# A one-core transformer layer with a mixture of experts: every token through every expert, or sorted rows through 72 expert tiles

## The reference

```python
scores = sigmoid(xf @ gate_w.T)                       # 8 experts
topk_w, topk_idx = top_k(scores, 2)
topk_w = topk_w / (topk_w.sum(-1) + 1e-20) * 2.5
shared_out = silu(xf @ shared_wg.T) * (xf @ shared_wu.T) @ shared_wd.T       # hidden width 352
h = silu(einsum('td,efd->etf', xf, exp_wg)) * einsum('td,efd->etf', xf, exp_wu)
all_out = einsum('etf,edf->etd', h, exp_wd)           # hidden width 176 per expert, all 8 experts
routed_out = (topk_w[..., None] * picked).sum(1)      # the two chosen of all_out
x = x + shared_out + routed_out
```

## Time and profile before

| | us |
|---|---|
| three runs, median (lowest to highest) | 6289.63 (6270.85 to 6297.65) |
| profiled execution, span from the first to the last instruction | 6271.0 |
| expert stage in it, 5590 to the end | 681 |
| of this: normalise, transpose, route | 5590 to 5630 |
| shared blocks | 5630 to 5766 |
| routed blocks | 5766 to 6271 |

### The profile page before, as it was taken

The page is one execution under the profiler, slowest core; times in us unless marked ns, Lnnn a source line. Parts: engine busy times, 40 slices in busy tenths (PEclk is TensorE's granted clock), DMA queues, the critical chain, the costliest instruction groups (busy, mean ns, idle before and its releaser), DMA issues. The chain is left out here.

```text
span 6271.0 us, 142359 instructions
## 1 busy us (share of the span) xinstructions
PE 4569.4 (73%) x49630; PEld 2127.3 (34%) x49630; DVE 5470.7 (87%) x7473; ACT 4790.6 (76%) x6674; POOL 4595.8 (73%) x3263
## 2 busy tenths in 40 slices
PE   7656666766667666666666667676666666899999
PEld 3422222222222222222222222222222224565555
DVE  8889999999999999999999999999999995543222
ACT  5469899998998898989998899898998993541010
POOL 4568888888888888888888888888888883530000
PEclk9889999999999999999999999999999998989999
DMA  4267777777777777777777777777777771010000
GB/s 126 66 125 144 137 142 144 140 143 138 146 143 139 140 146 140 142 146 140 142 142 157 140 143 140 141 142 138 143 144 143 140 145 45 0 36 0 9 8 10
DMA packets 2231975, 735.90 MB, mean 117 GB/s; under 512 B 2175765, under 2 KB 2209400, under 8 KB 2225561
## 3 DMA queue, kind: packets, MB, share of 16 engines
q1 hardware_dynamic: 2196249, 576.08, 45.2%
q0 software_dynamic: 35456, 157.33, 14.1%
HBM read 168.97 MB, written 27.26 MB: 31 GB/s over the span
## 5 line engine op out<-in xcount | busy, mean ns | idle before, releaser
L911 DVE TENSOR_SCALAR_CACHE_REDUCE scores<-ring,step 128x2048 f32<-128x2048 f32 (+2 forms) x2560 | 4780.0, 1919 | 51.5 <-PE ring L838 39.2
L970 ACT ACTIVATE n_op<-scores,bias 128x2048 uint8<-128x2048 f32 x2048 | 4075.9, 1997 | 279.0 <-DVE m_rest L918 278.8
L786 POOL CAST nT<-pairs 128x2048 f16<-128x2048 uint8 x2048 | 3790.9, 1890 | 515.9 <-DMA pairs<-n_op 504.8
L838 PE MATMUL ring<-x_all,q_op 128*128 128x512 bf16 x8192 | 2226.2, 385 | 652.9 <-DVE scores L911 589.1
L838 PEld LDWEIGHTS ring<-x_all,q_op 128*128 128x128 bf16 x8192 | 682.6, 98 | 1857.8 <-DVE scores L911 1186.2
L835 PE MATMUL ring<-x_all,q_op 128*128 128x512 bf16 x2048 | 628.8, 389 | 723.1 <-DVE scores L911 707.0
L850 PE MATMUL pO<-nT,v_op 128*32 128x128 f16 x32768 | 656.1, 223 | 148.4 <-ACT att_g L988 109.1
L850 PEld LDWEIGHTS pO<-nT,v_op 128*32 128x32 f16 x32768 | 479.4, 97 | 596.1 <-issue 513.4
L1760 ACT ACTIVATE h_gate<-pGt 128x512 f32<-128x512 f32 (+1 forms) x112 | 66.9, 597 | 528.3 <-PE pWt L1701 433.6
L835 PEld LDWEIGHTS ring<-x_all,q_op 128*128 128x128 bf16 x2048 | 116.6, 97 | 994.9 <-DVE scores L911 977.7
L970 ACT ACTIVATION_READ_ACCUMULATOR n_op<-scores,bias 128x1 f32 x2048 | 395.7, 193 | 0.0
(11 more groups left out here) (201 smaller groups left out, 3366.1 us busy)
## 6 DMA issues: line engine op xcount, KB each, us to landing
x_all<-keys_transposed POOLq DMA_DIRECT2D x128, 768.0 KB, 8.5
v_st<-value_integers POOLq DMA_DIRECT2D x128, 256.0 KB, 3.5
pairs<-n_op SPq DMA_TRANSPOSE x2048, 2.7
keys_transposed<-kT_s POOLq DMA_DIRECT2D x32, 384.0 KB, 3.3
cT<-in_ctx_T SPq DMA_DIRECT2D x32, 256.0 KB, 2.7
q_op<-queries_transposed POOLq DMA_DIRECT2D x384, 16.0 KB, 8.4
x_all<-in_x SPq DMA_DIRECT2D x1, 4096.0 KB, 16.8
value_integers<-v_int SPq DMA_DIRECT2D x1, 4096.0 KB, 13.0
```

Source lines behind the costliest of these rows:

```text
L786: nc.gpsimd.tensor_copy(nT[par][:, j * EK:(j + 1) * EK, :].rearrange("p (a c) b -> p a c b", c=2), src).then_inc(s_un, 1)
L838: mm = nc.tensor.matmul(slot(t, j)[:, n * BANK:(n + 1) * BANK], q_op[b][:, t * P:(t + 1) * P], k_op[b][:, at + n * BANK:at + (n + 1) * BAN ...
L911: nc.vector.tensor_scalar(score[t % 2][:, at:at + width * BANK], slot(t, j)[:, 0:width * BANK], step[b][:, t:t + 1], None, ALU.mult, ALU.m ...
L970: nc.scalar.activation(n_op[par][:, j * EW:(j + 1) * EW], score[par][:, j * EW:(j + 1) * EW], ACT.Exp, bias=bias[par][:], scale=-1.0, accu ...
```

## The change

The shared part stays as it is, but 5 of its 8 blocks run before the routed part and 3 behind it (FIRST = 5). The routed part no longer sends every token through every expert:

- DVE computes ranks in one go (`mark`), PE counts with two bf16 products how many tokens of each expert lie in earlier rows and tiles (`count`), and DVE makes from it for every token two slot numbers in an array sorted by expert, each expert's part padded to a multiple of 128 (`find_slots`), and for each of 72 tiles of 128 slots its expert (`find_experts`). 64 tiles hold the 8192 chosen rows, 8 are for the padding.
- POOL scatters the normalised tokens to HBM (`x_d`), one indirect DMA per token tile and pick: 64 of 128 rows x 1 KB. In the self attention block SP clears `x_d` first, 9 DMAs of 1 MB.
- For each of the 72 tiles PE transposes 128 slots (`turn_slots`), reads the tile's expert number from SBUF into a register, multiplies by this expert's gate and up weights (352 columns, `up_slots`), transposes the hidden rows (`turn_hidden`), and multiplies by its down weights (`down_slots`). SP loads slots and stores outputs in pairs of tiles, through two buffers each way.
- POOL gathers the two outputs of each token, again 64 indirect DMAs of 128 x 1 KB, the first 32 into free space, the other 32 as space comes free; DVE multiplies by the weight and adds; SP stores.

The core of the diff (declarations, `route`, `turn` and the unchanged forms of `up` and `down` are left out):

```diff
@@ self attention block
+            @block.sync
+            def _(sp):
+                ZT = 8
+                sp.wait_ge(s_id, 3)
+                for k in range(0, TILES, ZT):
+                    sp.dma_start(x_d[k * P:(k + ZT) * P, :].rearrange("(n p) d -> p n d", p=P),
+                                 zero_row[:].unsqueeze(1).to_broadcast([P, ZT, D])).then_inc(s_zf, 16)
+                sp.wait_ge(s_zf, 16 * (TILES // ZT))
@@ expert stage, sync
+                def load(j):
+                    if j >= XR:
+                        sp.wait_ge(s_zt, QT + PAIR * (j - XR + 1))
+                    sp.dma_start(xs[j % XR][:], x_d[j * PAIR * P:(j + 1) * PAIR * P, :].rearrange("(n p) d -> p n d", p=P)
+                                 ).then_inc(s_xs[j % XR], 16)
+                def store(j):
+                    sp.wait_ge(s_yc, PAIR * (j + 1))
+                    sp.dma_start(y_d[j * PAIR * P:(j + 1) * PAIR * P, :].rearrange("(n p) d -> p n d", p=P), ys[j % XR][:]
+                                 ).then_inc(s_ys[j % XR], 16)
+                sp.wait_ge(s_to, 16 * PICKS * QT)
+                for j in range(XR):
+                    load(j)
+                for j in range(NP):
+                    if j + XR < NP:
+                        load(j + XR)
+                    store(j)
+                for m in range(NBLK):
+                    sp.wait_ge(s_p2, TB * (m + 1))
+                    sp.dma_start(out_t[:, m * TB:(m + 1) * TB, :], x_all[:, m * TB:(m + 1) * TB, :]).then_inc(s_out, 16)
@@ gpsimd
+                pool.wait_ge(s_zn, QT)
+                pool.wait_ge(s_rs, 2)
+                for t in range(QT):
+                    for n in range(PICKS):
+                        pool.indirect_dma_start(
+                            out=x_d, out_offset=bass.IndirectOffsetOnAxis(ap=slot_of[:, n, t:t + 1], axis=0),
+                            in_=z_all[:, t, :], in_offset=None).then_inc(s_to, 16)
+                for i in range(XR):
+                    pool.wait_ge(s_ys[i], 16 * (NP // XR))
+                for t in range(QT):
+                    if t >= GR and t % GG == 0:
+                        pool.wait_ge(s_p2, t - GR + GG)
+                    for n in range(PICKS):
+                        pool.indirect_dma_start(
+                            out=picks[:, t % GR, n, :], out_offset=None, in_=y_d,
+                            in_offset=bass.IndirectOffsetOnAxis(ap=slot_of[:, n, t:t + 1], axis=0)
+                        ).then_inc(s_g[t % GR // GG], 16)
@@ tensor
+                for blk in range(FIRST):
+                    for f in range(NS):
+                        up(blk, f)
+                        if blk * NS + f == 1:
+                            count()
                     for t in range(TB):
+                        down(blk, t)
+                for k in range(-2, TILES + 1):
+                    if k + 2 < TILES:
+                        turn_slots(k + 2)
+                    if 0 <= k + 1 < TILES:
+                        chosen[k + 1] = pe.value_load(expert[0:1, k + 1:k + 2], min_val=0, max_val=E - 1)
+                        up_slots(k + 1, chosen[k + 1])
+                    if 0 <= k < TILES:
+                        turn_hidden(k)
+                    if k >= 1:
+                        down_slots(k - 1, chosen.pop(k - 1))
+                pe.wait_ge(s_yc, TILES)
+                for blk in range(FIRST, NBLK):
...
@@ scalar
+                def copy_slots(k):
+                    act.wait_ge(s_zt, QT + k + 1)
+                    nc.scalar.copy(xsT[k % 2][:], pTz[k % 2][:]).then_inc(s_zc, 1)
+                def activate_slots(k):
+                    act.wait_ge(s_ru, k + 1)
+                    nc.scalar.activation(r_gate[k % 2][:], pGt[k % 2][:, 0:W], ACT.Silu).then_inc(s_rg, 1)
@@ vector
+                mark()
+                shared(0, 0)
+                shared(0, 1)
+                find_slots()
+                for blk in range(FIRST):
...
+                for k in range(-1, TILES + 1):
+                    if 0 <= k + 1 < TILES:
+                        gated(k + 1)
+                    if 0 <= k < TILES:
+                        copy_hidden(k)
+                    if k >= 1:
+                        copy_output(k - 1)
+                for blk in range(FIRST, NBLK):
...
+                for t in range(0, QT, GG):
+                    dve.wait_ge(s_g[t % GR // GG], 16 * PICKS * GG * (t // GR + 1))
+                    dve.wait_ge(s_a, t + GG)
+                    for n in range(PICKS):
+                        for u in range(t, t + GG):
+                            sum_ = nc.vector.scalar_tensor_tensor(x_all[:, u, :], picks[:, u % GR, n, :],
+                                                                  weight[:, n, u:u + 1], x_all[:, u, :], ALU.mult, ALU.add)
```

More of the change, by code:

```diff
@@ L11 @@
 U8 = mybir.dt.uint8
+I32 = mybir.dt.int32
 F16 = mybir.dt.float16
@@ L1703, in up @@
                     mm.then_inc(s_up, 1)
-                def down(m, t, first, last, n):
-                    pe.wait_ge(s_a, after(m - 2))
-                    for j in range(first, last):
-                        if t == 0 and j >= last - 2:
-                            pe.wait_ge(s_h, after(n + j - first))
-                        lo, r = CHUNKS[j]
-                        mm = nc.tensor.matmul(pDn[t % 2], hidden[0:r, j, t * P:(t + 1) * P],
-                                              wd_sb[0:r, j, :], start=j == first, stop=j == last - 1)
-                    mm.then_inc(s_d, 1)
@@ new lines, in count, with turn_slots @@
+                def count():
+                    pe.wait_ge(s_bf, 8)
+                    pe.wait_ge(s_rs, 1)
+                    nc.tensor.matmul(p_before, earlier[:], member[:], start=True, stop=True)
+                    nc.tensor.matmul(p_total, ones_b[:], member[:], start=True, stop=True).then_inc(s_r, 1)
+                def turn_slots(k):
+                    pe.wait_ge(s_xs[k // PAIR % XR], slot_count(k // PAIR, XR))
+                    pe.wait_ge(s_zc, QT + k - 1)
+                    for c in range(DC):
+                        mm = nc.tensor.transpose(pTz[k % 2][:, c, :], xs[k // PAIR % XR][:, k % PAIR, c * P:(c + 1) * P],
+                                                 ident[:])
+                    mm.then_inc(s_zt, 1)
@@ new lines, in up_slots, with turn_hidden @@
+                def up_slots(k, e):
+                    pe.wait_ge(s_zc, QT + k + 1)
+                    for c in range(DC):
+                        mm = nc.tensor.matmul(pGt[k % 2][:, 0:2 * W], xsT[k % 2][:, c, :],
+                                              wgu_e[:, c].rearrange("p e n w -> p (e n w)")[:, bass.ds(e * (2 * W), 2 * W)],
+                                              start=c == 0, stop=c == DC - 1)
+                    mm.then_inc(s_ru, 1)
+                def turn_hidden(k):
+                    pe.wait_ge(s_rh, k + 1)
+                    for c in range(2):
+                        mm = nc.tensor.transpose(pHT[k % 2][:, c, :], r_hid[k % 2][:, c * HW:(c + 1) * HW], ident[:])
+                    mm.then_inc(s_rht, 1)
@@ new lines, in down_slots @@
+                def down_slots(k, e):
+                    pe.wait_ge(s_rhc, k + 1)
+                    if k >= 2:
+                        pe.wait_ge(s_yc, k - 1)
+                    for c in range(2):
+                        mm = nc.tensor.matmul(pDn[k % 2], r_hidT[k % 2][0:HW, c, :],
+                                              wd_e[0:HW].rearrange("p e c d -> p (e c d)")
+                                              [:, bass.ds(e * (2 * D) + c * D, D)], start=c == 0, stop=c == 1)
+                    mm.then_inc(s_rd, 1)
@@ new lines, in _ @@
+                shared(0, 0)
+                shared(0, 1)
+                find_slots()
+                for blk in range(FIRST):
+                    for f in range(NS):
+                        if blk > 0 or f > 1:
+                            shared(blk, f)
+                        if blk == 0 and f == 2:
+                            find_experts()
+                        if blk == 1 and f == 0:
+                            find_weights()
+                    for t in range(TB):
+                        add(blk * TB + t)
```

396 lines of the change are left out of this document (214 added, 182 removed).

## The result

The changed kernel takes 6111.6 us (median of 4 runs, 6106.2 to 6114.7); the kernel before, run beside it, 6283.4 (6270.9 to 6297.7, 4 runs). The ratio is 0.9724, with a 95% interval of 0.9706 to 0.9741: 2.8% faster. Forecast were 6136 us, in a range of 6050 to 6260. The profiled execution of after has a span of 6109.0 against 6271.0.

What follows compares the result with a forecast made beforehand. PE at full clock bounds the routed blocks (505 us). Of 320 us of PE work saved, 87 go to loads and reads, 5 front, 23 scatter and loop start, 52 tail: 153.9 less, 6136 us, range 6050 to 6260.

Steps and rivals of the forecast that it cites:

- The period of a pair: Routed loop, two tiles: the larger of 5.7 us of PE work and 7.55 through the load; 36 pairs make 272 us.
- The first tile's 3.1: PE time in us for a pair's first tile: 2.57 of work, 0.45 of shown register read, 0.1 for waits.
- The rest, 4.45 in the forecast: From the end of PE's turn through copy, SP's wake, store issue and load to PE's wake: 4.45 us.
- a cold start and a filling pipeline: Start of the routed loop: 4 us for PE's cold start and 6 for filling the pipeline.
- The read: PE's read of the tile's expert number: 0.7 us, 0.45 showing at a pair's first tile, hidden at the second.
- The gap: Between front and loop: PE idles, waiting for the scatter; first load lands 13 us after the front is through.
- The tail: Behind the loop: three shared blocks beside gathers, POOL waiting for DVE's late sums, then remaining gathers; 101.8 us.
- (a): Rival, routed loop: loads in time, store and load not delaying each other; period 5.7, time 6069 us; chance 0.10.
- (b): Rival, scatter and gather: indirect DMAs near their upper bound of 2.2 us each; time 6248 us; chance 0.12.
- (d): Rival, scatter and gather: row-by-row or serial indirect DMAs make POOL's queue the bound; 6414 us at 3.5 each; chance 0.13.
- the break-even: Scatter and gather: the time per indirect DMA at which 128 of them eat the whole saving, 2.5 us.
- (c): Rival, routed loop: PE's clock stays low, a tile takes 5.1 us, a pair 10.4; time 6238 us; chance 0.10.

Runs made afterwards that it cites:

- the first experiment: Early load: SP issues the load of pair j+3 ahead of the store of pair j, against the changed kernel; 6033.4 us, ratio 0.9613.
- the half scatter: Only 32 of the 64 scatters, each token's second choice not written, against the changed kernel; 6105.9 us (one run).
- the early sums: Load one pair earlier, plus DVE's first two groups of sums between the last shared blocks, against the changed kernel; 6012.1 us (one run).
- the second experiment: Fixed expert numbers in the program in place of PE's read, against the changed kernel; 6081.5 us, ratio 0.9661.
- the third experiment: Load one pair earlier and fixed expert numbers together, against the changed kernel; 6039.7 us (one run).
- the fifth experiment: PE's wait for hidden chunks put back at each chunk's own down product, against the changed kernel; 6101.9 us (one run).

## Why the prediction was right, step by step

**The mechanism held.** PE's work shrank to a tile's 2.49 us (forecast 2.57), the loads took PE's place as the bound, the scatter ended after the front, the sums held back the gathers. Each had its experiment: the first, the half scatter and the early sums. What was off are sizes. The stage came out 18 us shorter than forecast, of which the later start of the stage (10.1 us) hid a part in this profile. The time lies 24 us under the forecast: 8 are left of the 18, and 16 come from the median that I subtracted from, which lay 18.6 us above its profile's span, where after's lies 2.6 above.

**The period of a pair** was 7.26 us on average (31 steps from the load's issue at 5765.11 to that at 5990.32), forecast 7.55; the median of the slot transposes' steps is 7.03. Four of the 31 steps took 8.5 to 9.5 us, 7.3 us more than four of the others. In each of them the granted clock is at its low level for 3.4 us, at 5784.3, 5856.0, 5927.7 and 5978.9; two of them also had a slow load (3.42 and 3.59 us). So about 6 us of the loop are the clock's. The window of 10 us around the first of the four (mean clock 0.83), and how long the 36 loads took from issue to landing:

```profile
5780.00:5790.00 10.00, 7.72 (x27) 4.86 (x25) 2.81 (x9) 1.38 (x4) 0.00 (x0) 0.83 0.27 85
DMA to landing us min/median/max: 2.7/2.8/3.6
```

All five kernels in which PE waits for a load in every pair have two or four such falls in the loop. The four with the early load have none once the loop's first pairs are through. No experiment holds the waits and changes only the clock, so that the waits cause the falls is likely and not shown.

The first tile's 3.1 was met (5790.66 to 5793.77). The rest, 4.45 in the forecast, is the term that was mis-sized; a typical pair needs 3.9. The timeline of a pair in after:

```profile
5790.66 0.44 PE L1821 MATMUL pTz<-ident,xs 128*128 128x128 f32 x2 [0.77 <-DMA xs<-expert_slots_in]
5793.77 0.38 PE L1821 MATMUL pTz<-ident,xs 128*128 128x128 f32 x2
5793.97 0.42 DVE L2007 COPY ys<-pDn 128x256 f32<-128x256 f32 x1
5794.42 0.36 SPq L1727 DMA_DIRECT2D expert_slots_out<-ys  x1
5794.83 0.47 SPq L1722 DMA_DIRECT2D xs<-expert_slots_in  x1
5797.61 0.44 PE L1821 MATMUL pTz<-ident,xs 128*128 128x128 f32 x2 [1.18 <-DMA xs<-expert_slots_in]
```

SP's wake took 0.03 us (5794.39 to 5794.42) where I gave 0.3. The store ahead of the load cost about 0.1 (a median of 2.8 from issue to landing, 2.74 in this pair, against 2.7 for a quiet load) where I gave 0.4, and PE's wake 0.04 where I gave 0.1. Copy, store issue and load were as read. The surcharge for the store was the step of my own making: no row had it. PE's idle piece ahead of a pair was 1.3 us on average (42 us in 33 waits), forecast 1.9.

From the landing of the first load to the last copy the loop took 257 us, forecast 282. The shorter period makes 10 of the 25. The first three pairs took 14.1 us together and not three full periods, because their loads had been issued ahead of the first store: another 8. Of the 10 us for a cold start and a filling pipeline 3 were seen, in the last pair, which took 10.6 us from its transposes to its last copy; the other 7 did not come. That loads issued ahead would save periods at the start was missing in the forecast.

**The read** took 0.47 us, forecast 0.7. The mistake of substance is that I let the transposes cover 0.26 of it; the second experiment shows it late in full after a wait. So the part that shows, forecast 0.45 and measured 0.47, was met by two errors that cancel, which is luck. That a read under queued products costs nothing was right, as the third experiment shows, though it is the gate and up products that cover it.
The Trainium skill (DMA: Bandwidth & Descriptors, Latency and other measured facts) has about 600 ns as the floor of a tensor load; the 301 ns of a load here lie below it.

**Front.** The scatter started at +59.7 (forecast +58.2), PE waited for the ranks

```profile
5653.09 0.27 PE L1814 MATMUL pTz<-member,earlier 128*128 128x256 bf16 x1 [3.24 <-DVE member L1941]
```

as forecast (3 us). The front ended at +134.7, not +130.0: I took a block's 16.42 over from before and did not see that the down products now wait for all hidden chunks before the first one, 0.8 us a block, which the fifth experiment shows. So the shared part and its `down` did not stay as they were, as the description of the change has it. In front that costs nothing; behind the loop it does.

**The indirect DMAs.** Their spacing was forecast at 1.25 us. It was 1.29 in the scatter (63 steps from 5660.32 to 5741.43) and 1.28 in the gather behind the wait (31 steps from 6059.73 to 6099.46, most of them 1.25):

```profile
L1759 POOL DMA_INDIRECT expert_slots_in<-z_all,slot_of x64: 959/963/2180, 5660.3 to 5741.4; - x64
L1768 POOL DMA_INDIRECT z_all<-expert_slots_out,slot_of x64: 945/949/1272, 6006.7 to 6099.5; - x64
```

0.96 on POOL and 0.30 to the next. The gap was 12 us (forecast 13), the clock in it 0.70:

```profile
5746.75 1.09 PE L1821 MATMUL pTz<-ident,xs 128*128 128x128 f32 x4 [11.50 <-DMA xs<-expert_slots_in]
```

**The clearing** costs nothing that shows, as forecast. Its nine DMAs stand in the windows' last row (DMA share 1.04, 342 GB/s), where the self attention had next to none. From POOL's first product in the self attention (k_bd, L1375 before, L1392 in the others) to the stage's start it is 238.4 us before, and 237.3 to 239.5 in the nine kernels that clear. A version without the clearing wasn't tried.

**The tail** took 105.3 us against 101.8: POOL started 3.0 us after the loop as forecast, but the blocks took 17.2 us each, so the sums began later and POOL waited 13.2 and not 10.

```profile
6056.09 13.26 DVE L2042 SCALAR_TENSOR_TENSOR x_all<-z_all,weight,x_all 128x256 f32<-128x256 f32 x32
6102.28 3.38 DVE L2042 SCALAR_TENSOR_TENSOR x_all<-z_all,weight,x_all 128x256 f32<-128x256 f32 x8 [6.91 <-DMA z_all<-expert_slots_out,slot_of]
```

**The rivals.** (a), the loads are in time, fell: one edit that puts them in time gains 74 us. Its reason, though, was largely true: a store delays the load behind it by only 0.1 us. (b) and (d), a dear indirect DMA, fell by the 1.29 us above; the break-even was 2.5. The rule of the Trainium skill (GPSIMD Engine Reference, Performance pitfalls for Q7 kernels), by which I had estimated 10.9 us for 128 rows, does not describe this instruction: the trace has 0.96. (c), a clock that stays low, fell: the loop's window has 0.97 with PE waiting in every pair, and 0.99 in the first experiment, where it doesn't. But the clock was not near 1.00 throughout, as I had forecast: it had the four falls above. Four of a tile's eight matrix operations are transposes, and they did not keep the clock at the low level. So the rule of the Trainium skill (TensorE: Matmul & The Clock Gate, Part 4: PE-mode transpose) did not decide here.

**Where the PE time went that the change saves.** 72 tiles of 2.49 us are 179, against 505 before: 326 saved, of which the stage shows 172. Of the 154 between them, the loads, with the reads and the falls of the clock that go with them, took 74 (first experiment), the gap before the loop 12 (half scatter), and the tail behind the last shared block 53, of which 13 were the sums' order. The remaining 15 are put down, without an experiment for all of it, to the 3.2 us of waiting for the marks, 0.8 us in each of eight blocks, and the fill of the pipeline.

## What to carry to other kernels

When a kernel's bound is cut to a third, what fed it in its shadow becomes the bound: count, from the order of the code, how many turns lie between the issue of a load and its use, and compare that with the whole circle (copy, store, issue, landing); one turn more was worth 74 us here, nearly half of what the large change brought. A value read into a register was free behind queued work here and dear in full behind a wait, so measure waits before instructions. And compare stages from their own start, since a stage that starts up to 35 us earlier or later from one profile to the next hides any edit of 10.

## What the runs showed that I had not expected

- The stage's start differed by up to 35 us between profiles (5589.5 with the early sums, 5624.6 with the fixed expert) with the same arithmetic ahead of it. It arises in the cross attention; why that takes longer in one execution than in another stays open.
- The granted clock fell to its low level for 3.4 us at a time in the loops in which PE waits for a load in each pair (1.3 us on average in after), and not in those without the waits.
- An indirect DMA of 128 rows of 1 KB costs POOL 0.96 us, about what the direct DMA with 128x6 rows cost, and the first of the scatters 2.18.
- A load issued directly behind a store of the same size landed almost as early as a quiet one: a median of 2.8 us against 2.7.
- Semaphore hops took 0.02 to 0.04 us in the chain of a pair (the ends of PE's products are modelled there), a tenth of what I had read from one hop in the earlier trace rows.
